# Mixture of experts: routing weights through a scratch in DRAM instead of products with selectors

## What is computed

```python
shared_out = _silu_and_mul(xf @ shared_w1.T) @ shared_w2.T
probs = jax.nn.softmax(xf @ gate_w.T, axis=-1)                 # 16 experts
routing_weights, selected = jax.lax.top_k(probs, 6)
combine = zeros((T, 16)).at[arange(T)[:, None], selected].add(routing_weights)
act = _silu_and_mul(einsum('th,eoh->teo', xf, w1))             # 176 units for each expert
moe_out = einsum('te,tei,ehi->th', combine, act, w2)
x = x + moe_out + shared_out
```

## Time and profile before

| | us |
|---|---|
| median of 3 runs | 799.67 (798.83 to 799.82) |
| profiled execution | 799.59 |
| its span, first to last instruction | 797.8 |
| PE, DVE, ACT, POOL busy | 703.8, 469.2, 324.4, 248.0 |
| mean granted TensorE clock | 0.948 |

### The profile page before, as it was taken

How to read it: one execution, slowest core, us unless ns; L and a number is a source line. 1 busy time by engine, 2 the same in 40 slices (tenths; PEclk the granted TensorE clock), 3 DMA queues, 4 the chain that set the end, 5 groups by cost and what they waited for, 6 DMA issues and landing times.

```text
span 797.8 us, 11864 instructions
## 1 busy us (share of the span) xinstructions
PE 703.8 (88%) x4468; PEld 580.5 (73%) x4468; DVE 469.2 (59%) x1058; ACT 324.4 (41%) x773; POOL 248.0 (31%) x330
## 2 busy tenths in 40 slices
PE   4986599999888699867799998988599999999997
PEld 2764378788777588756677776766488888888886
DVE  4789777776437686564565546473654444444444
ACT  2424144554533233323676674664232222222221
POOL 1236510100324722314434432343423334333400
PEclk9989699999999799979899998999799999999999
DMA  6323000000112100000100000001111111111001
GB/s 215 100 66 97 14 1 1 2 1 1 47 37 63 44 18 21 1 20 24 38 1 2 2 1 1 1 2 39 39 28 53 41 40 40 51 48 41 1 1 53
DMA packets 11672, 25.82 MB, mean 32 GB/s; under 512 B 1344, under 2 KB 3392, under 8 KB 11584
## 3 DMA queue, kind: packets, MB, share of 16 engines
q1 hardware_dynamic: 11616, 25.07, 10.9%
HBM read 24.02 MB, written 1.05 MB: 31 GB/s over the span
## 4 chain that ended last, share of the span: by engine, by line
PE 71%; DVE 17%; ACT 5%; issue 4%; POOL 1%; DMA 1%; SPq 0%; DVEq 0%; ACTq 0%; POOLq 0%
PE ps L555 45%; PE ps L650 4%; PE ps L621 4%; PE ps L838 3%; PE ps L633 3%; PE ps L826 3%; PE ps L816 2%; DVE NB L1172 1%; PE ps L563 1%; ACT AO L1107 1%; PE ps L691 1%; PE ps L624 1%; PE ps L577 1%; DVE sml L1513 1%; ACT PB L1095 1%
## 5 line engine op out<-in xcount | busy, mean ns | idle before, releaser
L1696 POOL TENSOR_SCALAR PB<-PB,sml 128x256 f32<-128x256 f32 x128 | 59.1, 483 | 96.9 <-DVE sml L1530 96.9
L1024 ACT CAST VVh<-U 128x512 fp32r<-128x512 f32 x50 | 31.0, 620 | 128.0 <-PE ps L555 99.9
L1368 DVE TENSOR_TENSOR U<-U,ps 128x512 f32<-128x512 f32 x50 | 34.3, 687 | 73.9 <-PE ps L555 73.9
L555 PE MATMUL ps<-ATh,wh 128*128 128x512 f32 x176 | 72.5, 412 | 5.4 <-POOL wl L1667 2.5
L555 PE MATMUL ps<-ATh,wl 128*128 128x512 f32 x176 | 71.2, 405 | 0.0
L555 PE MATMUL ps<-ATl,wh 128*128 128x512 f32 x176 | 71.1, 404 | 0.0
L1665 POOL TENSOR_SCALAR wh<-wr 128x768 fp32r<-128x768 f32 (+3 forms) x31 | 24.1, 777 | 140.6 <-PE ps L555 140.4
L1095 ACT ACTIVATE PB<-ps,sml 128x256 f32<-128x256 f32 x128 | 59.5, 492 | 12.7 <-DVE sml L1524 12.7
L1380 DVE TENSOR_TENSOR VVl<-U,VVh 128x512 fp32r<-128x512 f32 x50 | 40.5, 811 | 36.9 <-ACT VVh L1024 36.9
L650 PEld LDWEIGHTS ps<-VK,PT 128*128 128x128 f32 x384 | 49.3, 191 | 12.0 <-issue 11.4
L1667 POOL TENSOR_TENSOR wl<-wr,wh 128x768 fp32r<-128x768 f32 (+3 forms) x31 | 55.6, 1793 | 2.6
(11 more groups left out here) (257 smaller groups left out, 2051.7 us busy)
## 6 DMA issues: line engine op xcount, KB each, us to landing
wr<-in_w SPq DMA_DIRECT2D x32, 384.0 KB, 3.1
wr<-in_w SPq DMA_DIRECT2D x16, 321.0 KB, 3.0
wr<-in_w SPq DMA_DIRECT2D x11, 256.0 KB, 2.6
XO<-in_x SPq DMA_DIRECT2D x2, 512.0 KB, 4.7
out_dram<-XO SPq DMA_DIRECT2D x8, 128.0 KB, 1.7
wr<-in_w SPq DMA_DIRECT2D x2, 416.0 KB, 6.1
AO<-in_sm SPq DMA_DIRECT2D x1, 448.0 KB, 7.3
SELf<-in_sel SPq DMA_DIRECT2D x1, 352.0 KB, 3.9
```

The source lines that it names most:

```text
L555: t = x.matmul(o, a, b, start=first and i == 0 and c == 0, stop=last and i == n - 1 and c == 2, skip_group_check=skip)
L1368: x.tensor_tensor(b[:, :], a[:, :], bank("u", run, j, half)[:, :], ALU.mult).then_inc(*vacates("u", run, j, half))
L1696: t = x.tensor_scalar(p[:, c, :], p[:, c, :], m[:, 16 + c:17 + c], 1.0, ALU.mult, ALU.mult)
```

## The change

The selector matrix, its buffers and POOL's `selector` item go, and so does the product of line 691 with its PSUM bank. The turned weights are kept as plain float32, 16 rows in place of 32, with no high and low part, which takes three short DVE operations from `route`. SP writes each half of `CTr` to a scratch in DRAM (`routes`, 16 rows of 1024) and waits for it; then, for each step of j 3 or more, it reads the rows of the chunk's experts back, each repeated to the partitions of its units, into one of six buffers `CB` of 128x512. DVE's second multiply reads that buffer instead of the PSUM bank. A chunk that holds units of two experts takes two such reads; 14 of the 22 do. SP issues them in program order between the weight loads: before the load of chunk n, all that have j + 3*half of at most n-6, and the rest after the last load.

```diff
+NSPREAD = 6
@@ plan
-    item("selector")
@@ buffers
-    chr_ = sb("chr", [128, NT, 16], R32)
-    cl = sb("cl", [128, NT, 32])
+    cl = sb("cl", [128, NT, 16])
-    SELf = sb("SELf", [32, 22 * 128], ctx=m1)
-    SELr = sb("SELr", [128, 22 * 128], R32, ctx=m1)
-    CTr = sb("CTr", [128, T], R32, ctx=m1)
+    CTr = sb("CTr", [16, T], ctx=m1)
+    routes = nc.dram_tensor("weights_of_experts", (16, T), F32, kind="Internal").ap()
+    CB = [sb(f"CB{i}", [128, 512], ctx=m1) for i in range(NSPREAD)]
+    gated = [tuple(o[2:]) for o in order if o[0] == "step" and o[1] == "moe" and o[2] >= 3]
@@ tensor: step
-            if run == "moe" and j >= 3:
-                b = fills(ring["w"], "c", run, j, half)
-                e.wait_ge(*at("selr"))
-                e.wait_ge(*vacated("sp", half))
-                x.matmul(b[:, :], SELr[:, (j - 3) * 128:(j - 2) * 128], CTr[:, sl], start=True, stop=True).then_inc(
-                    *filled("c", run, j, half))
@@ scalar: spread
-            e.wait_ge(*at("blank"))
+            if half == 0:
+                for s in latent_end():
+                    e.wait_ge(*s)
             e.wait_ge(*have("sp", half))
-            x.copy(CTr[0:32, half_cols(half)], bank("sp", half)[0:32, :]).then_inc(*vacates("sp", half))
+            x.copy(CTr[:, half_cols(half)], bank("sp", half)[0:16, :]).then_inc(*vacates("sp", half))
@@ vector: step
-                    e.wait_ge(*have("c", run, j, half))
+                    k = gated.index((j, half))
+                    e.wait_ge(*at(f"spread{k % NSPREAD}", k))
                     e.wait_ge(*vacated("u", run, j, half))
-                    x.tensor_tensor(b[:, :], b[:, :], bank("c", run, j, half)[:, :], ALU.mult).then_inc(
-                        *vacates("c", run, j, half))
-                    S.value["hid", run, j, half] = vacated("c", run, j, half)
+                    x.tensor_tensor(b[:, :], b[:, :], CB[k % NSPREAD][:, :], ALU.mult).then_inc(*mark("gated", k))
+                    S.same(("hid", run, j, half), ("gated", k))
@@ sync
+        sent = [0]
+
+        def spread():
+
+            k = sent[0]
+            j, half = gated[k]
+            sent[0] += 1
+            if j == 3:
+                e.wait_ge(*vacated("sp", half))
+                x_.dma_start(routes[:, half_cols(half)], CTr[:, half_cols(half)]).then_inc(*mark("routed", half, by=16))
+            e.wait_ge(*at("routed", half))
+            if k >= NSPREAD:
+                e.wait_ge(*at("gated", k - NSPREAD))
+            first = (j - 3) * 128
+            for x0 in range(first // 176, (first + 127) // 176 + 1):
+                a, b = max(x0 * 176, first) - first, min(x0 * 176 + 176, first + 128) - first
+                src = routes[x0:x0 + 1, half_cols(half)].to_broadcast([b - a, 512])
+                x_.dma_start(CB[k % NSPREAD][a:b, :], src).then_inc(
+                    *mark(f"spread{k % NSPREAD}", k, by=16))
@@ sync: the loads
         for name, _, _ in CHUNKS[NRAW:]:
-            if name == "moe5":
-                for s in latent_end():
-                    e.wait_ge(*s)
-                x_.dma_start(SELf[:, :], sel).then_inc(*mark("sel", by=16))
+            if name.startswith("moe"):
+                while sent[0] < len(gated) and gated[sent[0]][0] + 3 * gated[sent[0]][1] <= int(name[3:]) - 6:
+                    spread()
             load(name)
+        while sent[0] < len(gated):
+            spread()
```

More of the change, by code:

```diff
@@ L873, in spread @@
             for c in range(4):
-                p = x.transpose(b[0:32, c * 128:(c + 1) * 128], cl[:, half * 4 + c, :], ident)
+                p = x.transpose(b[0:16, c * 128:(c + 1) * 128], cl[:, half * 4 + c, :], ident)
             p.then_inc(*filled("sp", half))
@@ L1584, in route @@
             e.wait_ge(*now("dv"))
[L1585 to L1593, removed]
+            x.scalar_tensor_tensor(out=cl[:, hs, :], in0=rp[:, hs, 0:16], scalar=0.0, in1=pr[:, hs, 0:16], op0=ALU.is_lt,
+                                   op1=ALU.mult).then_inc(*mark("rt", half))
         def store(t):
@@ L1701, in endnorm @@
             rsqrt(rs, ve, half, "ve4", "rs4")
-        def selector():
-            for s in latent_end():
-                e.wait_ge(*s)
[L1706 to L1710, removed]
         run(order, {"norm1": norm1, "rotate": rotate, "mask": mask, "l0begin": l0begin, "split": split, "memnorm": memnorm,
                     "memturn": memturn, "ffnmean": ffnmean, "expert": expert, "latstd": latstd, "l1norm": l1norm,
-                    "endnorm": endnorm, "selector": selector})
+                    "endnorm": endnorm})
     def sync(x_):
```

## The result

The changed kernel takes 935.6 us (median of 4, 928.5 to 936.0) against 799.75: 1.168 times as long, interval 1.162 to 1.174. Forecast were 927 us, 885 to 985. Its profiled execution took 935.4 us, the span 933.6.

A forecast was written before the change was run, and what follows sets the result against it. PE bounded the kernel before; late reads would then form a cycle. moe6's split at 597.8 + 16 x 16.9 = 868.2, +130.7 on that point, less 3.0 for thirteen steps, turned 799.6 into 927 us; range 885 to 985.

The forecast's parts named there:

- The ring: Last block, half 0: late reads close a cycle from D(i-4,1) to D(i-3,1), paid 16 times, i = 4 to 19.
- The cycle, 16.9 us: Each turn in half 0: 0.3 + 2.9 + 4.0 + 2.3 + 5.65 = 15.2 us, plus 1.7 for the clock.
- the landing: Within each cycle: the read lands 4.0 us after the load's issue; low end 2.9, high end 5.5.
- DMA: Load and read in each cycle: skill figures gave 3.5 us, 8 us less in all; the trace's 4.0 was used.
- The clock, 1.7 us for a cycle: After PE's 6.7 us standstill in each cycle: some 3.3 us at half rate lose 1.7 us; ends 0 and 5.65.
- The start: Start of last block: D(0,0) 4.2 us sooner without POOL's selector work; moe6's split at 597.8 against 593.76.
- The tail and PE's share: After the cycles, thirteen steps of 0.23 us save 3.0; 44 selector products off PE save 10.3 if PE bounds.
- Rivals 3 and 4: Half 0's cycle shorter (900 or 882 us, chance 0.14) or longer (951, 990 or 1014 us, chance 0.17).
- The factor of three for one repeated row: CB reads in half 0: 128 reads of one row might go at a third of the rate, 1.5 us more.
- rival 4: Longer cycle: slow one-row reads (951 us), most of PE's part at half clock (990), or both (1014); chance 0.17.
- The signs to look for: Half 0: DVE waits for reads, PE waits 6.7 us per D(i,0), splits 16 to 17 us apart, clock near 0.8.

The follow-up runs named there:

- reads_two_earlier: The changed kernel with each read of routing weights two weight loads earlier in SP's list: 784.3 us, 0.981 of the kernel before.
- late_until_12: The changed kernel with reads in the late place up to the load of moe17, two loads earlier after it: 875.3 us, 1.095.
- plain_read: The changed kernel with each read as one DMA of 128 different rows of the weights instead of one row repeated: 931.8 us.
- busy_wait_28: The changed kernel with 28 unused products of 512 columns on PE ahead of D(i,0), i = 4 to 19: 908.6 us, 1.135.
- clears_back_nogap: `reads_two_earlier` with POOL's two clearings, without a wait between them, and its rounding put back on an unused buffer: 789.0 us, 0.985.
- splits_after_low: `reads_two_earlier` with POOL's splits of moe3 and moe4 held until DVE has made the low part for D(0,0): 777.1 us, 0.970.
- clears_back: `reads_two_earlier` with POOL's two clearings, a wait between them, and its rounding put back on an unused buffer: 785.7 us, 0.982.

## Why the prediction was right, point by point

- **The ring.** Right: reads behind a load that waits for a D before them, 16 cycles, then PE as the bound again. `reads_two_earlier` shows that the place makes the loss, `late_until_12` that each cycle is paid.
- **The cycle, 16.9 us.** Measured 17.33, in these terms (forecast in brackets): split to the load's issue 2.79 (2.9); load's issue to DVE's start 4.58 (4.0); DVE to D(i,0) 2.18 (2.3); D(i,0) to the next split 7.79 (5.65 + 0.3 + 1.7 = 7.65). The mis-sized term is the landing, 0.6 us or 10 us over 16 cycles. I had taken one read of 256 KB in a single piece of different rows; `plain_read`, which is just that, lands after 3.88. The second piece (0.3) and the repeated row (0.4) were the rest. Two of the other terms came 0.1 us short and one 0.1 us long, and the cycle is 0.4 us over the forecast's, 7 us over 16 cycles; the start gave 1.2 more.
- **DMA.** From the figures of the Trainium skill (DMA: Bandwidth & Descriptors, Anatomy of one DMA) I had an estimate of 3.5 us for load and read. That section gives them for DMAs that GpSimd issues, while SP issues these. Even `plain_read`'s 3.88 is above the estimate; the measurement decides.
- **The clock, 1.7 us for a cycle.** Right: 7.79 against 6.11 us behind D(i,0)'s start in `busy_wait_28`, and the loss returned in every turn. The Trainium skill's rule (TensorE: Matmul & The Clock Gate, HAM oscillation — how this bites in real kernels) agrees with the trace, 0.79 over the 16 cycles. What I had not seen is that it isn't a constant added to the cycle: `plain_read` shows it growing as PE's wait shrinks. That the size fits is in part luck: at a landing near the forecast 4.0 us, which `plain_read` has, the term is 8.22 - 6.11 = 2.1 us and the cycle 17.07, not 16.9.
- **The start.** The split of moe6 was forecast at 597.8 and came at 599.0; the first read took 3.3 us from its issue to DVE's start, forecast 2.6. D(0,0)'s wait went from 10.3 to 5.98 us, 4.3 against 4.2. The step was right with its reason, as `clears_back_nogap` shows, and incomplete: it took POOL's splits for harmless, and they cost another 7 us, 784.3 against 777.1 in `splits_after_low`.
- **The tail and PE's share.** From the split of moe22's place to the end 57.2 us, where the kernel before has 60.3: 3.0 less, as thirteen products of 0.23. `reads_two_earlier` is 15.3 us below 799.6. The 10.3 for the 44 products, 4.3 at the start and 0.7 for a wait of PE at 597, which the kernel before alone has, add up to that, but the fit is luck, for they leave out terms of the same size: the kernel before runs at the lower clock from 584.5 to 587.9 us (1.7 us lost) and `reads_two_earlier` does not; after D(0,0) the lower level lasts 3.2 us in the kernel before and 5.7 in `reads_two_earlier` (1.3 us lost by it); and in the latter's trace the block begins 1.3 us later. What the products are worth is read in mid-block, where a chunk takes 8.45 us, forecast 8.44.
- **Rivals 3 and 4** described the right mechanism with other sizes. A clock that stays up would have given 900; `busy_wait_28`, which forces it, has 908.6, by the longer landing. The factor of three for one repeated row was far off; it is at most 0.4 us. Its price was also reckoned too low: by the increment that the prediction used, 1.0 us for 256 KB, a third of the rate is 2.0 us more and not 1.5, 959 us and not 951. And the upper end of the range, 985, leaves out rival 4's 990, though the text says that the range takes in the clock's end.
- **The signs to look for.** Multiply waiting for the read, PE's wait of 6.9 us on average before each D(i,0) (6.7 forecast) and 110.6 in all, splits 17 us apart, clock near 0.8: all there. The read's landing from its own issue was 3.9 us for 256 KB, 3.6 forecast.

## What to carry to other kernels

A DMA is issued no sooner than the wait ahead of it in its issuing queue ends. Before costing the transfer, write down which wait stands in front of it and whether that wait depends on the work that needs the data. If it does, the lateness is a ring and is paid in every turn; compare issue time and need for one step in the middle of the loop, and leave room for the landing, the issues of its pieces and a write that must come first. A product that only prepares data costs the distance between starts, not its row's duration: 0.23 us here, and moving it off PE was worth that only with the reads in time.

## What the runs showed of the hardware

- A cycle with a long PE wait in it held a length of 17.07 us while its data came 0.4 us earlier: the clock was at its lower level for 6.83 us in each cycle either way, and after the shorter wait more of PE's work fell into that stretch (4.7 instead of 3.9 us). Small gains in such a loop can vanish in the clock.
- The clock fell after PE waits as short as 1.85 us, with PE already at work again, and held through waits of up to 1.7 us in the same loop. Length alone does not decide: in the kernel before, the clock was at its lower level from 584.5 to 587.9 us although PE had not stood still since 567.6; from 580.5 to 583.1 it had done 24 products of 16 columns. What decides was not tried.
- DVE's normalising of 128x256 from SBUF, 0.41 us alone, did not run beside POOL's splits or clearings at the start of the last block and got in only between two POOL operations; a pause of 0.06 us between two clearings decided over 2.4 us (the fourth operation took 2.85 with it and 5.24 without). The low part, with two SBUF inputs, took 1.7 to 2.3 us beside a POOL operation that reads SBUF and had begun before it, and 0.69 beside the clearing of `clears_back`, which reads nothing. The Trainium skill (SBUF — State Buffer, SBUF: two separate sides) states both: an exclusive hold of a shared port for a whole instruction, which for DVE operations with two SBUF inputs applies only against a GpSimd operation that reads SBUF. The traces agree. For the normalising, which has one tile as input, the section asks for a mode of DVE that uses both ports; no run here shows the mode.
- Reading one row of 2 KB from DRAM to 128 partitions took 3.9 us from issue to landing, 128 different rows of another tensor 3.5, both as medians over 44 reads, 16 of them right behind a load.
